# Attention and FFN on eight cores: heads and output tiles transposed by DMA, the first slab shared by four head pairs, side work planned by length

## The chip, the cores and the metric

The kernel runs on the eight NeuronCores of one Trainium2 chip. The cores work alone: no data passes between them. A core has TensorE (PE, matrix products), VectorE (DVE), ScalarE (ACT, here the exponentials), GpSimd (POOL) and SyncE (SP), each with its own instruction queue, and DMA queues that SP, POOL and ACT feed. Engines wait for each other by semaphores only. The metric is the device time of the slowest core, in microseconds.

## The reference, cut to what matters

```
x: (4, 4096, 1024)                      # 16 heads of width 64; one key and one value head for all
r = layernorm(x)
q = r @ query_proj   (per head)   k = r @ key_proj   v = r @ value_proj
o = softmax(q k^T / 8) v                # each head, 4096 keys
x = x + o @ output_proj
r = layernorm(x)
s = r @ Win + bin                       # 64 channels
g[m] = sum over h of relu(s[m] * W1[m,h] + b1[m,h]) * W2[m,h] + b2[m]     # 16 inner units
out = x + g @ Wout + bout
```

## The kernel before, in words

Two cores share one of the four sequences. Each computes keys and values for all 4096 rows (its own 2048, then the other core's), and outputs for its own. Matrices are bf16, sums f32.

The keys come in 32 tiles of 128 rows, four to a slab. A tile is loaded into `xbuf` (tiles 4 to 7 into `xtra`), DVE takes its statistics (`ln_stats`, L465), POOL makes 1/sqrt(var) in two steps (`rstd_of`, L833), DVE writes the normed bf16 tile `r1u` (`ln_norm`, L473), TensorE transposes it in eight 128x128 pieces into one of two side banks of PSUM (`sda`, `sdb`), and DVE copies it to `r1t`. A slab then gives keys (`K`, eight 512-column matmuls), values (`V`, 32 of 64 columns) and, for the core's own first four slabs, queries (`Q`, eight matmuls for a pair of heads). The core's 2048 queries are four stages k of 512; the 16 heads are eight pairs hp.

The main loop has 1024 groups. Group g takes one key tile, one head pair and 512 queries: two score matmuls on 64 rows (L662) into `spa` or `spb`, one exponential of 128x1024 on ACT (L816) into `ptu`, and eight P·V matmuls of 65 columns (L457; the 65th is the row sum) into `ob`. TensorE issues the scores of g+2 when exponential g is done, then P·V of earlier groups, eight or twelve at a time (`pv_at`). A slot is what stands on TensorE between the scores of one group and those of the next. `SEGS` (L32) is the order of the groups: stage 0 goes through the slabs as they come (the sums of a head pair are kept in `oacc` and DVE adds to them), stages 1 to 3 take each pair through all 32 tiles. At a pair's last group DVE normalises its output into `on` (`o_out`, L716).

All else is side work: a list `USES` (L120) of transposes (`tr`), keys, values, queries, transposed heads (`ot`: `on` to `ot`), output projections (`op`, `oq`), transposed output tiles (`rt`, from `r1u` to `r2t`), the FFN's first product (`s2`) and its second (`fo`). Each use takes the side bank that the use before last held, so TensorE waits at it for DVE's evacuation (`wait_ev`, semaphore `sev`). `pace` (L138) plans where the pieces stand among the groups, while the program is built: 2, 1 or 0 pieces in a slot with 0, 8 or 12 P·V matmuls, one DVE piece a slot, and, ahead of scores or P·V that need a key, value or query, everything up to it at once ("forced"). Engines run in order, so a piece that waits holds the scores behind it.

Stage k's projection and FFN run as side work of stage k+1. The last two output tiles are finished after the last exponential (the tail: `oq` leaves their last two head chunks to it). Result tiles are stored from POOL's queue, the next x tiles loaded from SP's (L895).

## Time and profile before

| | |
|---|---|
| median of 3 runs (lowest to highest) | 1017.74 us (1017.22 to 1017.86) |
| profiled execution, its own time | 1017.6 us |
| span of its slowest core; all cores | 1016.1 us; 1012.9 to 1016.1 us |
| ACT busy | 952.2 us, 94% of the span |
| PE busy, weight loads | 900.6 us (89%), 493.1 us (49%) |
| DVE busy | 358.7 us, 35% |
| granted clock of TensorE, all cores | 0.986 to 0.989 |

Busy time is the share of the span in which an engine had an instruction in work. ACT's exponentials overlap in the records: one is shown as lasting up to 1.2 us, while they start 0.9 us apart. The profiled execution's time is 1.5 us more than its slowest core's span, which is what lies around the program.

### The profile page before, as it was taken

What the parts mean: (1) busy time and instruction counts of PE and PEld (TensorE: products, weight loads), DVE (VectorE), ACT (ScalarE), POOL (GpSimd) and SP (SyncE); (2) the same over time, 40 slices, a digit from 0 to 9 for tenths busy, and PEclk for the clock granted to TensorE, in tenths of its full rate; (3) what the DMA queues carried; (4) which work ended last, traced back from release to release, by engine and by line L of the source; (5) the groups of instructions that cost most, each with busy time, mean ns of one, the idle gap of its engine ahead of it and who ended that gap; (6) DMA issues with size and microseconds to landing.
All of it is one profiled execution on the core that took longest, in us unless ns stands there. A gap on an engine that the chain in (4) does not pass through costs nothing.

```text
span 1016.1 us, 28595 instructions; the slowest of 8 cores (1012.9 to 1016.1 us)
## 1 busy us (share of the span) xinstructions
PE 900.6 (89%) x11582; PEld 493.1 (49%) x11712; DVE 358.7 (35%) x637; ACT 952.2 (94%) x1043; POOL 56.5 (6%) x131
## 2 busy tenths in 40 slices
PE   3898899998899999998889999998889998898884
PEld 3445555555444545544444454544444554454442
DVE  4535666652512222234202122244202326424215
ACT  2597999999999999999999999999999999999981
POOL 3201111100000000000000000000000000000000
...
GB/s 196 138 12 85 85 119 174 85 85 3 1 2 2 2 2 2 2 2 84 85 2 2 1 3 1 2 2 62 58 51 2 2 2 2 167 2 1 44 2 41
DMA packets 13406, 40.94 MB, mean 40 GB/s; under 512 B 3168, under 2 KB 3296, under 8 KB 13152
## 3 DMA queue, kind: packets, MB, share of 16 engines
...
q10 hardware_dynamic: 288, 0.52, 0.1%
...
## 4 chain that ended last, share of the span: by engine, by line
ACT 80%; issue 9%; PE 5%; DVE 3%; DMA 3%; POOL 0%; DVEq 0%; SPq 0%; POOLq 0%; ACTq 0%
ACT ptu L816 80%; DMA xtra<-x_own 2%; PE ob L457 1%; DMA xbuf<-x_own 1%; PE spa L662 1%; PE spb L662 1%; DVE r1u L478 1%; PE sda L380 0%; DVE r1t L504 0%; DVE lnst L468 0%; PE spb L695 0%; DVE lnst L469 0%; DVE gacc L787 0%; POOL rstd L838 0%; PE sdb L391 0%
## 5 line engine op out<-in xcount | busy, mean ns | idle before, releaser
L816 ACT ACTIVATE ptu<-spa 128x1024 bf16<-128x1024 f32 x512 | 594.5, 1161 | 17.7 <-PE spa L662 17.6
L816 ACT ACTIVATE ptu<-spb 128x1024 bf16<-128x1024 f32 x512 | 595.9, 1164 | 2.9 <-PE spb L662 2.9
L457 PE MATMUL ob<-vab,ptu 128*128 128x65 bf16 x8192 | 409.1, 195 | 0.7 <-ACT ptu L816 0.5
L457 PEld LDWEIGHTS ob<-vab,ptu 128*128 128x128 bf16 x8192 | 298.4, 97 | 208.4 <-issue 208.4
L662 PE MATMUL spb<-qt,k2t 64*128 64x512 bf16 x1024 | 200.8, 380 | 40.5 <-ACT ptu L816 34.9
L662 PE MATMUL spa<-qt,k2t 64*128 64x512 bf16 x1024 | 200.9, 380 | 36.5 <-ACT ptu L816 28.3
L662 PEld LDWEIGHTS spb<-qt,k2t 64*128 64x128 bf16 x1024 | 63.4, 92 | 127.2 <-issue 108.1
L662 PEld LDWEIGHTS spa<-qt,k2t 64*128 64x128 bf16 x1024 | 62.6, 92 | 114.5 <-issue 95.1
L725 DVE TENSOR_TENSOR oacc<-oacc,ob 128x520 f32<-128x520 f32 x50 | 34.8, 696 | 77.3 <-PE ob L457 77.2
L836 POOL TENSOR_SCALAR lnve<-lnmv 128x1 f32<-128x1 f32 x48 | 12.7, 264 | 658.0 <-DVE lnmv L471 658.0
L527 DVE TENSOR_TENSOR xbuf<-xbuf,sda 128x512 f32<-128x512 f32 x16 | 11.0, 688 | 93.3 <-PE sda L423 80.0
L527 DVE TENSOR_TENSOR xbuf<-xbuf,sdb 128x512 f32<-128x512 f32 x16 | 11.0, 688 | 89.5 <-PE sdb L423 54.9
L732 DVE RECIPROCAL zrec<-ob 128x8 f32<-128x8 f32 x24 | 5.0, 207 | 100.1 <-PE ob L457 99.8
L478 DVE TENSOR_SCALAR r1u<-xbuf,lnmv,rstd 128x1024 bf16<-128x1024 f32 x44 | 35.6, 810 | 9.1 <-POOL rstd L838 9.1
L423 PE MATMUL sda<-xtra,ot 128*128 128x512 bf16 x98 | 37.0, 379 | 0.0
L402 PE MATMUL sdb<-r1t,wqb 128*128 128x512 bf16 x104 | 35.9, 380 | 0.1
L423 PE MATMUL sdb<-xtra,ot 128*128 128x512 bf16 x96 | 35.4, 379 | 0.2 <-issue 0.2
L513 DVE CAST qt<-sdb 128x512 bf16<-128x512 f32 x16 | 11.0, 690 | 69.5 <-PE sdb L402 40.8
L402 PE MATMUL sda<-r1t,wqb 128*128 128x512 bf16 x96 | 34.4, 380 | 0.1
L468 DVE BATCH_NORM_STATS2 lnst<-xbuf 128x6 f32<-128x512 f32 x44 | 30.3, 689 | 10.9 <-DMA xbuf<-x_own 7.7
L513 DVE CAST qt<-sda 128x512 bf16<-128x512 f32 x15 | 10.3, 690 | 61.4 <-PE sda L402 42.9
L469 DVE BATCH_NORM_STATS2 lnst<-xbuf 128x6 f32<-128x512 f32 x44 | 29.7, 676 | 0.0
...
## 6 DMA issues: line engine op xcount, KB each, us to landing
xbuf<-x_own SPq DMA_DIRECT2D x28, 512.0 KB, 4.4
xbuf<-x_oth SPq DMA_DIRECT2D x16, 512.0 KB, 3.9
out<-xbuf POOLq DMA_DIRECT2D x14, 512.0 KB, 3.6
wqb<-wq POOLq DMA_DIRECT2D x8, 256.0 KB, 9.6
xtra<-x_own SPq DMA_DIRECT2D x4, 512.0 KB, 6.9
...
boutbc_s<-boutbc SPq DMA_DIRECT2D x1, 512.0 KB, 12.7
out<-xbuf SPq DMA_DIRECT2D x2, 256.0 KB, 2.6
```

What stands on the lines that cost most here:

```text
L402: r = te.matmul(bank[:], wqb[:, b, j, :], r1t[:, a, j, :], start=(j == 0), stop=(j == DCH - 1))
L423: r = te.matmul(bank[:], ot[:, blk % 2, c, t * 128:(t + 1) * 128], wpb[:, c, b * 512:(b + 1) * 512], start=(c == 0), stop=(c == heads - 1))
L457: r = te.matmul(osum[:, hd, c * 65:(c + 1) * 65], ptu[:, g % NPT, hd * 512 + c * 128:hd * 512 + (c + 1) * 128], vab[:, a + i, :], start=(i ...
L468: v.bn_stats(lnst[:, q, 0:6], xt(li)[:, 0:512])
L469: v.bn_stats(lnst[:, q, 6:12], xt(li)[:, 512:1024]).then_inc(bns, 1)
L478: v.tensor_scalar(r1u[:, li % 2, :], xt(li), lnmv[:, q, 0:1], rstd[:, q, :], op0=ALU.subtract, op1=ALU.mult).then_inc(nrm, 1)
L513: v.tensor_copy(qt[:, a % 2, b, :], bank[:]).then_inc(sev, 1)
L527: v.tensor_tensor(xh, xh, bank[:], op=ALU.add).then_inc(sev, 1)
L662: mm = te.matmul(sps[g % 2][:, hh * 512:(hh + 1) * 512], k2t[rows, mc * 128:(mc + 1) * 128], q, start=True, stop=True)
L725: v.tensor_tensor(oacc[:, hp], oacc[:, hp], osum, op=ALU.add).then_inc(oev, 1)
L816: sc.activation(ptu[:, g % NPT, :], sps[g % 2][:], AF.Exp, scale=0.125).then_inc(ex, 1)
L836: e.tensor_scalar(lnve[:, q, :], lnmv[:, q, 1:2], EPS, None, op0=ALU.add).then_inc(veps, 1)
```

## The change

1. Order of groups: head pairs 0 to 3 (before: 0 and 1) each go through slab 0 before slab 1 is used; pairs 4 to 7 then take both slabs at once. V0 comes ahead of the first scores; the queries of pairs 1 to 4 alternate with the transposes of slab 1; the keys of slab 1 are made in two pieces of 384 and 128 columns.
2. `r1u` has four buffers instead of two. Key tiles are transposed by TensorE as before.
3. Heads and output tiles are transposed by DMA on SP's queue (`head_transpose`, `tile_transpose`), in the order in which the plan notes them, except the very last head pair and the two tiles of the tail. Heads of stage 3 go in two halves. TensorE waits for their landing (`otl`, `trl`) at `op`, `oq` and `s2`; DVE waits before it writes a buffer of `on` or `r1u` again.
4. `pace` counts lengths in hundredths of a microsecond: a slot is 92, scores 22, half a P·V group 12, a piece 22, and pieces are added while TensorE's lag stays at or under 25. DVE's pieces have lengths too. A transposed head or tile counts as there six slots after its source.
5. The queries of stage 1 come at the end of stage 0, those of stage k+1 in stage k. The x tiles of later stages are loaded from POOL's queue, behind the stores; the projection's weights in eight loads instead of one.

```diff
-SEGS = [(0, 0, 0, 4), (0, 1, 0, 4), (0, 0, 4, 8), (0, 1, 4, 8)]
-SEGS += [(0, hp, 0, 8) for hp in range(2, NHP)]
+SEGS = [(0, hp, 4 * sl, 4 * sl + 4) for sl in range(2) for hp in range(4)]
+SEGS += [(0, hp, 0, 8) for hp in range(4, NHP)]
 SEGS += [(0, hp, 4 * sl, 4 * sl + 4) for sl in range(2, NSLAB) for hp in range(NHP)]
...
+    tr = slab(1)
+    o = [("V", 0, 0)] + q(0, 1) + tr[:1] + q(0, 2) + tr[1:2] + q(0, 3) + tr[2:3] + q(0, 4) + tr[3:]
+    o += [("V", 1, 0)] + q(0, 5, 6, 7)
     for s in range(2, NSLAB):
         o += slab(s) + [("V", s, 0)]
-    return o + q(1, 0) + [("ot", 0, hp) for hp in range(NHP - 1)]
+    return o + q(1, *range(NHP))
 
 
 def output_parts(b):
 
...
     fo = [("fo", 4 * b + t, h) for t in range(4) for h in range(2)]
-    return [op[0], op[1], rt[0:1] + op[2], rt[1:2] + op[3], rt[2:4], [("s2", b, 0)], fo[0:4], fo[4:8]]
+    return op + [[], [("s2", b, 0)], fo[0:4], fo[4:8]]
 
...
+SLOT = 92
+SCORES = 22
+SWITCH = 20
+HALF = 12
+PIECE = 22
+PE_LAG = 25
+TR_LAG = 6
...
+    def force(want, where):
+        n = 0
+        while not ok(want, -TR_LAG):
+            mm = [("smd", v) for name, v in want if name == "sev"]
+            if not ok(mm, 0) and ok(head["pe"], -TR_LAG):
+                run("pe", pe, "pe" + where)
+                n += 1
+            else:
+                assert head["dve"] is not None and ok(head["dve"][0], -TR_LAG), (now, head)
+                run("dve", dve, "dve" + where)
+        return n
+
+    pe_lag = dve_lag = 0
...
+            if last_part(s):
                 note("onr", 8 * SEGS[s][0] + SEGS[s][1] + 1)
-        while not ok(want, 0):
-            if head["pe"] is not None and ok(head["pe"], 0):
-                run("pe", pe, "pe0")
-            else:
-                assert head["dve"] is not None and ok(head["dve"], 0), (g, head)
-                run("dve", dve, "dve0")
+                note("otd", 8 * SEGS[s][0] + SEGS[s][1] + 1, TR_LAG)
...
+        forced += force([("sev", USE_NO["V", (SEGS[s][2] + h // 2) // 4, 0] + 1) for h in halves], "_v")
+
+        pe_lag = min(pe_lag + PIECE * forced, PE_LAG)
+        t = SCORES + HALF * len(halves) + (SWITCH if halves or forced else 0)
+        switch = 0 if halves or forced else SWITCH
+        while head["pe"] is not None and ok(head["pe"], 1):
+
+            if pe_lag + t + switch + PIECE - SLOT > (PE_LAG if g >= 14 else 75):
+                break
+            run("pe", pe, "pe")
+            t += switch + PIECE
+            switch = 0
+        pe_lag = max(0, pe_lag + t - SLOT)
+
+        room = SLOT + (20 if g + 1 in SEG_AT else 115)
+        while head["dve"] is not None and ok(head["dve"][0], 1) and dve_lag + head["dve"][1] <= room:
+            dve_lag += head["dve"][1]
+            run("dve", dve, "dve")
+        dve_lag = max(0, dve_lag - SLOT)
+    return counts, moves
 
 
...
+                                         r1u[:, a % 4, j * 128:(j + 1) * 128], identb[:])
                 elif kind == "K":
-                    yield [("sev", n)]
-                    wait_ev(te, n - 1)
-                    for j in range(DCH):
-                        if j:
-                            yield []
-                        r = te.matmul(bank[:], wkb[:, j, :], r1t[:, slab_buf(a), j, :],
-                                      start=(j == 0), stop=(j == DCH - 1))
+
+                    parts = [(0, 3), (3, 4)] if a == 1 else [(0, 4)]
+                    for t0, t1 in parts:
+                        tr = USE_NO["tr", 4 * a + t1 - 1, 0]
+                        cols = slice(128 * t0, 128 * t1)
+                        for j in range(DCH):
+                            if j == 0:
+                                yield [free, ("sev", tr + 1)]
+                                wait_ev(te, n - 2)
+                                wait_ev(te, tr)
+                            elif j % (4 if t1 - t0 == 1 else 1) == 0:
+                                yield []
+                            r = te.matmul(bank[:, cols], wkb[:, j, :], r1t[:, slab_buf(a), j, cols],
+                                          start=(j == 0), stop=(j == DCH - 1))
                 elif kind == "V":
                     yield [free]
...
-                    yield [free, ("sev", done + 1)]
+
+                    done = 8 * blk + ({12: 3, 14: 6}[a // 2 * 2] if blk == LAST else NHP - 1)
+                    yield [free, ("otd", done + 1)]
...
+                    li = NTILES + GROUPS[a][-1]
+                    yield [free, ("trd", li + 1)]
                     if a == 0:
                         te.wait_ge(winl, 16)
-                    wait_ev(te, n - 1)
+                    wait_ev(te, n - 2)
...
 
 
-        def ln_stats(v, li):
+        def ln_stats_a(v, li):
             q = li % 4
             wait_x(v, li)
             v.bn_stats(lnst[:, q, 0:6], xt(li)[:, 0:512])
+
+        def ln_stats_b(v, li):
+            q = li % 4
...
-            if 2 <= li < 6:
-                v.wait_ge(ptr, li - 1)
-            v.tensor_scalar(r1u[:, li % 2, :], xt(li), lnmv[:, q, 0:1], rstd[:, q, :],
+            if 4 <= li < 8:
+                v.wait_ge(ptr, li - 3)
+            elif li < NTILES + 4:
+
+                if li >= 8:
+                    v.wait_ge(smd, USE_NO["tr", li - 4, 0] + 1)
+            else:
...
                 r.then_inc(kmm, 1)
-            te.wait_ge(pset, 1)
-            te.wait_ge(qev, 2)
             for g in range(-2, NG):
-                run(gen, counts["pe0"].get(g, 0))
+                run(gen, counts["pe_s"].get(g, 0))
+                if g == -2:
+                    te.wait_ge(pset, 1)
+                    te.wait_ge(qev, 2)
...
+                    v.wait_ge(otl[n % 2], heads_moved(n - 2))
                 v.reciprocal(zrec[:, n % 2], src[:, :, :, 64:65]).then_inc(rcp, 1)
...
+                    c = i - 24
                     e.wait_ge(nrm, 8)
-                    e.dma_start(wpb, wp_d.rearrange("p (c d) -> p c d", d=D)).then_inc(wpl, 16)
+                    e.dma_start(wpb[:, c, :], wp_d[:, c * D:(c + 1) * D]).then_inc(wpl, 16)
             for ts in GROUPS[:-1]:
                 for t in ts:
...
+                        e.wait_ge(ost[t % 4], 16 * (t // 4 + 1))
+                        e.dma_start(xbuf[:, t % 4, :], xo_r[t + 4]).then_inc(xol[t % 4], 16)
             for t in GROUPS[-1]:
                 rstd_of(e, NTILES + t)
...
+        def tile_transpose(e, li, dst):
+            e.wait_ge(nrm, li + 1)
+            e.dma_start_transpose(dst, r1u[:, li % 4, :]).then_inc(trl[li % 4], 16)
+
+        def head_transpose(e, k, i):
+
+            n = 8 * k + i
+            if i == 0 and k >= 2:
+                wait_ev(e, USE_NO["op", 4 * (k - 2) + 3, 1])
+            e.wait_ge(onr, n + 1)
+            if k < LAST:
+                e.dma_start_transpose(ot[:, k % 2, i, :].rearrange("p (c t) -> p c t", c=4),
+                                      on[:, n % 2].rearrange("p c t -> p (c t)")).then_inc(otl[n % 2], 16)
+            else:
+                q0 = 256 * (i // 4)
+                for c in range(2):
+                    e.dma_start_transpose(
+                        ot[:, k % 2, 2 * (i % 4) + c, q0:q0 + 256].rearrange("p (c t) -> p c t", c=2),
+                        on[:, n % 2, 2 * c:2 * c + 2].rearrange("p c t -> p (c t)")).then_inc(otl[n % 2], 16)
 
         @block.sync
         def _(e):
@@ -892,10 +986,15 @@
...
-                for t in range(4):
-                    e.wait_ge(ost[t], 16 * k)
-                    e.dma_start(xbuf[:, t, :], xo_r[4 * k + t]).then_inc(xl[t], 16)
+            for kind, n in moves:
+                if kind == "otd":
+                    if n < 8 * NK - 1:
+                        head_transpose(e, n // 8, n % 8)
+                    continue
+                t = n - NTILES
+                if t == GROUPS[GROUP_OF[t]][0]:
+                    wait_ev(e, USE_NO["s2", GROUP_OF[t] - 1, 0] if t else USE_NO["V", 6, 0])
+                tile_transpose(e, n, r2t[:, :, t % 4 * 128:t % 4 * 128 + 128])
             for n, t in enumerate(GROUPS[-1]):
                 e.wait_ge(oad, 2 * n + 1)
                 e.dma_start(out_r[t][:, 0:512], xbuf[:, t % 4, 0:512]).then_inc(osp, 16)

```

TensorE's queue at the start, ahead of the first scores that need slab 1; before (L662 scores, L457 P·V, L372 transposes, L380 keys, L391 values, L402 queries):

```order
L662 MATMUL spb<-qt,k2t 128x512 x2
L457 MATMUL ob<-vab,ptu 128x65 x12
L372 MATMUL sdb<-identb,r1u 128x128 x8
L372 MATMUL sda<-identb,r1u 128x128 x8
L372 MATMUL sdb<-identb,r1u 128x128 x8
L380 MATMUL sda<-r1t,wkb 128x512 x8
L391 MATMUL sdb<-wvb,r1t 128x64 x32
L662 MATMUL spa<-qt,k2t 128x512 x2
L457 MATMUL ob<-vab,ptu 128x65 x12
L662 MATMUL spb<-qt,k2t 128x512 x2
L457 MATMUL ob<-vab,ptu 128x65 x8
```

After, the piece of head pair 3 that ends in the first scores of slab 1 (L727 scores, L513 P·V, L453 queries, L415 transposes, L430 keys):

```order
L453 MATMUL sdb<-r1t,wqb 128x512 x2
L727 MATMUL spa<-qt,k2t 128x512 x2
L453 MATMUL sdb<-r1t,wqb 128x512 x4
L727 MATMUL spb<-qt,k2t 128x512 x2
L513 MATMUL ob<-vab,ptu 128x65 x12
L453 MATMUL sdb<-r1t,wqb 128x512 x2
L415 MATMUL sda<-identb,r1u 128x128 x8
L430 MATMUL sdb<-r1t,wkb 128x384 x8
L430 MATMUL sdb<-r1t,wkb 128x128 x8
L727 MATMUL spa<-qt,k2t 128x512 x2
```

What stood ahead of the ninth group's scores stands ahead of the seventeenth's. The values have gone behind them, and queries of the next pair have come in between.

TensorE's queue ahead of slab 2; before (row L380 is the key matmul of slab 2):

```order
L372 MATMUL sda<-identb,r1u 128x128 x4
L662 MATMUL spa<-qt,k2t 128x512 x2
L457 MATMUL ob<-vab,ptu 128x65 x8
L372 MATMUL sda<-identb,r1u 128x128 x4
L662 MATMUL spb<-qt,k2t 128x512 x2
L457 MATMUL ob<-vab,ptu 128x65 x8
L372 MATMUL sdb<-identb,r1u 128x128 x8
L380 MATMUL sda<-r1t,wkb 128x512 x8
L391 MATMUL sdb<-wvb,r1t 128x64 x32
L662 MATMUL spa<-qt,k2t 128x512 x2
```

After, the keys of slab 2, which begin eleven groups before the sixty-fifth group's scores:

```order
L430 MATMUL sda<-r1t,wkb 128x512 x2
L727 MATMUL spa<-qt,k2t 128x512 x2
L513 MATMUL ob<-vab,ptu 128x65 x8
L430 MATMUL sda<-r1t,wkb 128x512
L727 MATMUL spb<-qt,k2t 128x512 x2
L513 MATMUL ob<-vab,ptu 128x65 x8
L430 MATMUL sda<-r1t,wkb 128x512
L727 MATMUL spa<-qt,k2t 128x512 x2
L513 MATMUL ob<-vab,ptu 128x65 x8
L430 MATMUL sda<-r1t,wkb 128x512
L727 MATMUL spb<-qt,k2t 128x512 x2
L513 MATMUL ob<-vab,ptu 128x65 x8
```

The keys of slab 2 and its values have moved from one slot into a dozen.

DVE's queue in the new start, between the query cast of pair 1 and that of pair 2 (L583 query casts, L789 copy of the sums, L574 copy of a transposed tile, L524 to L530 statistics, L547 norm):

```order
L583 CAST qt<-sdb 128x512 [waits sem_side_mm]
L789 COPY oacc<-ob 128x520 [waits sem_pv_mm]
L574 COPY r1t<-sda 128x8x128 [waits sem_side_mm]
L524 BN_STATS lnst<-xtra 128x6 [waits sem_xtra_load2]
L528 BN_STATS lnst<-xtra 128x6
L530 BN_AGGR lnmv<-lnst 128x2 [waits sem_bn_stats]
L547 TENSOR_SCALAR r1u<-xtra,lnmv,rstd 128x1024 [waits sem_rstd_set,sem_first_transposed]
L583 CAST qt<-sdb 128x512 [waits sem_side_mm]
```

The cast of the next query stands behind a tile's statistics and another's norm; in the old order these stood among transposes.

## Rows read from the trace of the kernel before

**Rows 1.** The page: the chain that ended last, shares of the span by engine.
```profile
ACT 80%; issue 9%; PE 5%; DVE 3%; DMA 3%; POOL 0%; DVEq 0%; SPq 0%; POOLq 0%; ACTq 0%
```

**Rows 2.** ACT's waits (total us, times, longest), 24 to 62 us, then 62 to 1000.
```profile
ACT ptu L816 <- PE spa L662: 10.4, 4, 6.6
ACT ptu L816 <- PE spb L662: 1.9, 1, 1.9
...
ACT ptu L816 <- PE spa L662: 7.1, 3, 6.3
ACT ptu L816 <- PE spb L662: 1.0, 2, 0.8
```

**Rows 3.** ACT in order of time: start us, duration us, instruction [idle before].
```profile
24.18 1.02 ACT L816 ACTIVATE ptu<-spa 128x1024 bf16<-128x1024 f32 x1 [0.32 <-PE spa L662]
...
51.27 1.02 ACT L816 ACTIVATE ptu<-spa 128x1024 bf16<-128x1024 f32 x1 [2.06 <-PE spa L662]
...
93.27 1.20 ACT L816 ACTIVATE ptu<-spa 128x1024 bf16<-128x1024 f32 x1
94.18 1.20 ACT L816 ACTIVATE ptu<-spb 128x1024 bf16<-128x1024 f32 x1
101.67 1.02 ACT L816 ACTIVATE ptu<-spa 128x1024 bf16<-128x1024 f32 x1 [6.29 <-PE spa L662]
...
984.56 1.20 ACT L816 ACTIVATE ptu<-spb 128x1024 bf16<-128x1024 f32 x1
```

**Rows 4.** All engines in order of time, 22 to 27 us: the first scores, V0.
```profile
22.88 0.61 PE L635 MATMUL ob<-r1t,wkb 128*128 128x128 bf16 x8
...
23.70 0.39 PE L662 MATMUL spa<-qt,k2t 64*128 64x512 bf16 x2 [0.20 <-DVE qt L756]
...
25.68 1.11 PE L391 MATMUL sda<-wvb,r1t 128*128 128x64 bf16 x32
```

**Rows 5.** All engines, 38 to 42 us, and two rows near 87 us.
```profile
38.56 1.67 PE L380 MATMUL sda<-r1t,wkb 128*128 128x512 bf16 x7 [1.16 <-DVE r1t L504]
...
40.34 0.69 DVE L508 CAST k2t<-sda 128x512 bf16<-128x512 f32 x1 [2.14 <-PE sda L380]
...
41.29 0.39 PE L662 MATMUL spa<-qt,k2t 64*128 64x512 bf16 x2
...
41.62 0.54 PE L457 MATMUL ob<-vab,ptu 128*128 128x65 bf16 x12
...
42.09 0.39 PE L662 MATMUL spb<-qt,k2t 64*128 64x512 bf16 x2
...
86.68 0.42 PE L457 MATMUL ob<-vab,ptu 128*128 128x65 bf16 x8
...
86.94 0.39 PE L372 MATMUL sda<-identb,r1u 128*128 128x128 bf16 x4
```

**Rows 6.** The page's groups: busy us, mean ns of one, idle before.
```profile
L402 PE MATMUL sdb<-r1t,wqb 128*128 128x512 bf16 x104 | 35.9, 380 | 0.1
...
L468 DVE BATCH_NORM_STATS2 lnst<-xbuf 128x6 f32<-128x512 f32 x44 | 30.3, 689 | 10.9 <-DMA xbuf<-x_own 7.7
...
L478 DVE TENSOR_SCALAR r1u<-xbuf,lnmv,rstd 128x1024 bf16<-128x1024 f32 x44 | 35.6, 810 | 9.1 <-POOL rstd L838 9.1
```

**Rows 7.** The page's DMA issues: count, KB each, us from issue to landing.
```profile
xbuf<-x_own SPq DMA_DIRECT2D x28, 512.0 KB, 4.4
...
wqb<-wq POOLq DMA_DIRECT2D x8, 256.0 KB, 9.6
```

**Rows 8.** A stretch: us, PE, PEld, DVE, ACT, POOL busy, PEclk, DMA share, GB/s.
```profile
95.00:102.00 7.00, 5.02 (x51) 2.93 (x52) 4.80 (x10) 0.71 (x2) 1.56 (x4) 0.76 0.15 60
```

**Rows 9.** All engines: the keys of slab 2; the last P·V; the last norm.
```profile
96.98 3.00 PE L380 MATMUL sda<-r1t,wkb 128*128 128x512 bf16 x7 [2.10 <-DVE r1t L504]
...
985.90 0.41 PE L457 MATMUL ob<-vab,ptu 128*128 128x65 bf16 x8 [0.52 <-ACT ptu L816]
...
986.73 0.69 DVE L734 TENSOR_TENSOR on<-ob,zrec 128x512 bf16<-128x512 f32 x1
```

184 lines of the change are left out of this document (92 added, 92 removed).

## The prediction

> **What bounds the kernel now.** The page's head gives the slowest core a span of 1016.1 us, in an execution of 1017.6 us; 80% of the chain that ended last is the exponential of line 816 on ACT [rows 1]. Before a share is trusted, the stage behind it is to be read: the exponentials stand 0.91 to 0.92 us apart when nothing disturbs them (93.27 to 94.18), the first starts at 24.18, the last at 984.56 [rows 3]. 1024 of them at that step are 939 us, and no part of the change touches the step. What is left is 24 us ahead of the first, 30 us behind the last, whose code is the same but for buffer indices, and the holes. ACT's waits say where those are: 10.4 + 1.9 us before 62 us, 7.1 + 1.0 us after it [rows 2]. In order of time the reader sees two places: the seventeenth exponential (slab 1 is done by then) starts at 51.27, where a hole-free run would have it at 24.18 + 14.7 = 38.9; and the sixty-fifth, the first that needs slab 2, comes 7.49 us after its predecessor, 6.3 of them idle [rows 3]. All other holes are 7.1 + 1.0 - 6.3 = 1.8 us. So at most 20.4 us can be had, whatever DVE and PE shed elsewhere.
>
> **The change, part by part.**
> *V0 ahead of the first scores.* The first scores started at 23.70, having waited for a query cast [rows 4]. The key matmuls before them started at 22.88 and take 0.61 - 0.17 = 0.44 of TensorE's time (0.17 is what one 512-column matmul's 0.38 [rows 6] is over the step of 0.21 that seven in 1.67 show [rows 5]). V0's 32 matmuls then run from 23.3 for 1.11 - 0.17 = 0.94 [rows 4], the scores start at 24.3, and the first exponential 0.48 later: 24.8, +0.6.
> *First slab used by four head pairs.* Per pair the new order on TensorE, by the steps of [rows 5]: scores 0.33 (41.29 to 41.62) four times, twelve P·V twice 0.47 (41.62 to 42.09), eight P·V 0.26 (86.68 to 86.94), eight transposes 0.5, eight query matmuls 1.7, the last one's end 0.17: 4.9 us. The next pair's scores wait for that query's cast: 0.1, then 0.69, and 0.26 until TensorE goes on (40.34 + 0.69 to 41.29). DVE is later still: ahead of that cast stand the copy of the sums, the transposed tile's copy, statistics (two at 0.69 and an aggregate, 1.6) and a norm (0.81) [rows 6], 3.8 us that can begin 1.5 us after the scores, so the cast starts at 5.3 instead of 5.0. A period is 6.3 us for four exponentials, where their own time is 3.7. The first pair: the scores of its fourth key tile wait for five query matmuls, those of pair 1 for DVE, which has two tiles of statistics and a norm before the cast (24.5 + 0.4 + 3.2 + 0.8 + 0.7 + 0.3 = 29.9): the fifth exponential is at 30.4. The ninth 36.7, the thirteenth 43.0. Then TensorE's queue holds the last transposes and both pieces of key matmuls: 5.0 + 0.7 + 0.3 for the query's cast, 8 x 0.16 for 384 columns, 0.44 for 128, 0.2, cast 0.69, 0.26, to which 0.2 comes for the hop: 8.8, so the seventeenth is at 51.8. Before: 51.27. So this part loses 0.6 in all, V0 included: the four pairs give work to ACT, but each query is asked for just before its use. Unknown is what late weights do: query chunk 3 is issued near 27.8 and needed at 38.1, 10.3 us for a transfer whose median is 9.6 [rows 7]; from nothing to 2 us.
> *V1.* 24 matmuls (0.7) and then P·V that waits for their cast: 0.8 in place of 0.33. Two slots take 2.3 against 1.83; an exponential after a hole lasts 1.02 and in the steady stretch 1.20 [rows 3], so 0.18 of lateness is free. +0.3.
> *Slab 2 planned.* In the order of before, eight transposes, eight key and 32 value matmuls stand in one slot ahead of the scores that need slab 2. In the new order they are spread from slot 40 to 62, the last key matmul six slots before its use. The 6.3 us go. What is late next there is nothing I find: 8 P·V with one piece is 0.33 + 0.26 + 0.21 = 0.8, below 0.917. Of the 1.8 us in other holes, made by the same kind of forced pieces, I take 1.0 as gained; bounds 0 and 1.8.
> *Pieces by length.* From slot 16 on there are now 79 slots with 12 P·V and a piece (none before) and 75 with 8 P·V and two (one with more before). They cost 0.33 + 0.47 + 0.21 = 1.01 and about 0.33 + 0.26 + 0.43 = 1.02, 0.1 over a slot; the plan's own lag may reach 0.25, 0.07 beyond the free 0.18. No row has such a slot, so bounds: nothing, since lighter slots follow, and 75 x 0.07 = 5 us. I take 0.3, near the lower end, because the lag counted is seldom at its top.
> *Heads and output tiles by DMA.* 31 head and 14 tile transposes leave TensorE and DVE; both wait for ACT in those stages, so this brings nothing. What replaces them are 52 transposing transfers on SP's queue (38 of heads, those of stage 3 in halves, and 14 of tiles), in the order of the plan; SP stands still at each until its source is written, and behind it only further transposes wait, the loads of x having gone to POOL's queue. POOL there holds the next tiles' rstd behind the stores' landing and four loads, each about the 4.4 us of a 512 KB load [rows 7], with over 30 slots before that rstd is wanted. The price is a wait on TensorE, with scores queued behind it. The last P·V of a stage stands 8 slots (7.3 us) before the first projection; reciprocal and norm end 1.1 after that P·V's 0.41 (985.90 to 987.42 [rows 9]), and in stage 0 the sum costs another 0.8. That leaves 5.4 us once (stage 0) and 6.2 four times. Tiles: 5.9 before the third FFN and 5.0 before the fourth (11 and 9 slots less 4.2 and 3.2, with POOL's two steps and hops estimated at 1.1), over 10 before the others. A head is 128 KB, a tile 256 KB. The nearest rows are plain loads of 512 KB at 4.4 and, in the crowd of the start, 9.6 for half that [rows 7]. I take 4.4 as the likelier, since in these stages the queues are near empty: no wait. The other end, 9.6, costs 4.2 + 4 x 3.4 + 3.7 + 4.6 = 26 us.
> The Trainium skill disagrees with itself here. "VectorE: DVE Perf Modes", section "The three transpose paths", gives the DMA crossbar 1.31 us for 128x128 where TensorE has 0.39. If blocks add up, an estimate from that page is 5.2 us for a head and 10.5 for a tile. "DMA: Bandwidth & Descriptors", section "Anatomy of one DMA", gives a fixed 2 us and the bytes at 436 GB/s; an estimate by that is 2.3 and 2.6 us, and then no wait at all. No row here shows a transposing transfer; by the first page the sum would be rival C, by the second the forecast.
>
> **Sum.** +0.6 (start) + 0.3 (V1) - 6.3 (slab 2) - 1.0 (small holes) + 0.3 (heavy slots) + 0 (transfers) = -6.1. The profiled execution was 1017.6, so 1011.5; the median of the runs is 0.1 above it: 1011.7 us. The unknowns at their best (all small holes, DVE 0.5 earlier in each of the first periods, heavy slots nothing) give 1009; and if the start hides one more cast, 1007.5.
>
> **Rivals.**
> A. The start costs more than worked out: a query's weights land 2 us late, or TensorE's granted clock falls in the first 52 us. For it: it fell in the hole before slab 2, to 0.76 on the mean of 95 to 102 [rows 8], and the new start has gaps of 1.3 us in each period. Against: the larger hole before 41 us cost no clock. In that stretch the seven key matmuls took 3.00 [rows 9] where 1.67 is usual [rows 5], so 1.3 per such fall. Time: 1011.7 + 2 to 3, 1014.
> B. The heavier slots are not absorbed: +5 as bounded above, 1016.5. For it: 154 such slots. Against: none exceeds a slot by more than 0.1.
> C. Slower: transposing transfers outlast the plan. With one length L for all, the seven close waits cost (L - 5.4) + 4(L - 6.2) + (L - 5.9) + (L - 5.0) = 7L - 41; that passes the gain of 6.1 from L = 6.7. At twice the plain load, 8.8, it is 20.5 and the time 1032. It is worse if they also don't overlap, for the heads of stage 0 come every 3.7 us: at 5.2 each, the last of eight lands 11 us late, DVE waits for the buffer of normed heads, and with tiles at 10.5 (4.6 + 5.5) the sum is +21, again 1032. For it: no row of this kernel shows such a transfer at all. Against: twice to four times the bytes land in 4.4.
> D. The change doesn't remove the wait for slab 2 but meets it elsewhere, since the same 48 exponentials must cover the same tiles. Against: slots 16 to 62 have 36 us and the pieces need under 25. It is taken with A.
>
> **Chances.** Forecast 0.66 (its own range 1009 to 1014), A with D 0.14, B 0.07, C 0.13. A measurement tells 0.2%, 2.0 us, from no change. Faster by more: all but a little of the forecast, two thirds of A, a quarter of B: 0.77. Same: 0.10. Slower: C, 0.13. The range reaches up over A and B to 1018.5 and down to 1007.5; C is left out.
>
> **What would show it.** The first exponential at 24.8, the fifth near 30.4, the seventeenth near 51.8; no hole over 1 us at the sixty-fifth; the last near 978.5; holes by ACT's waits near 14 in all; head transfers under 5.4 us from issue to landing and no wait of TensorE at the first projections; steady step 0.917 still. It would be wrong if the seventeenth came 3 us from 51.8, if the step in the middle stages grew, or if a transposing transfer took over 6 us.

## The result, and the profile after

The changed kernel takes 1029.54 us (median of 4 runs, 1028.76 to 1029.84); the kernel before took 1017.74 in the same comparison. The ratio is 1.0116 with an interval of 1.0096 to 1.0136: slower by 11.8 us, where 6.1 us less had been forecast. The profiled execution has a span of 1027.2 us on its slowest core (all cores 1020.5 to 1027.2), 11.1 more than before. Some executions of any kernel run with the cores of one die at a lower clock and take some per cent longer; the times and ratios of this document leave them out.

The chain of the page, by engine, answers to [rows 1]; the two groups of exponentials follow (busy us, mean ns of one, idle before).

```profile
ACT 47%; PE 34%; issue 8%; DVE 7%; DMA 2%; DVEq 0%; SPq 0%; POOL 0%; ACTq 0%; POOLq 0%
...
L885 ACT ACTIVATE ptu<-spa 128x1024 bf16<-128x1024 f32 x512 | 552.7, 1079 | 19.5 <-PE spa L727 17.6
L885 ACT ACTIVATE ptu<-spb 128x1024 bf16<-128x1024 f32 x512 | 553.2, 1081 | 2.9 <-PE spb L727 2.8
```

ACT has 47% of the chain where it had 80%, PE 34% where it had 5%. And an exponential's mean duration fell from 1.16 us (the mean over the trace of before) to 1.08. That is bad news here: the records of neighbours overlap while ACT has the next one waiting, so a short record is one that was fed late.

ACT's waits, from 24 to 62 us and from 62 to 1000, answer to [rows 2].

```profile
ACT ptu L885 <- PE spa L727: 12.2, 9, 4.6
ACT ptu L885 <- PE spb L727: 1.1, 4, 0.3
...
ACT ptu L885 <- PE spa L727: 5.4, 11, 1.7
ACT ptu L885 <- PE spb L727: 1.7, 7, 0.3
ACT ptu L885 <- issue: 0.8, 4, 0.2
```

Behind 62 us the waits are 7.9 us where they were 8.1. By this view nothing was lost there. The starts of the exponentials tell another story. In order of time, answering to [rows 3]:

```profile
25.10 1.02 ACT L885 ACTIVATE ptu<-spa 128x1024 bf16<-128x1024 f32 x1 [1.46 <-PE spa L727]
...
52.63 1.02 ACT L885 ACTIVATE ptu<-spa 128x1024 bf16<-128x1024 f32 x1 [4.58 <-PE spa L727]
...
96.61 1.07 ACT L885 ACTIVATE ptu<-spb 128x1024 bf16<-128x1024 f32 x1
97.70 1.03 ACT L885 ACTIVATE ptu<-spa 128x1024 bf16<-128x1024 f32 x1
...
995.51 1.09 ACT L885 ACTIVATE ptu<-spb 128x1024 bf16<-128x1024 f32 x1
```

The hole ahead of slab 2 is gone: 97.70 is the sixty-fifth exponential, 1.09 behind its predecessor instead of 7.49. Counting exponentials from 0, the two kernels compare so, each in its slowest core:

| stretch | before, us | after, us | difference |
|---|---|---|---|
| span's start to exp 0 | 24.18 | 25.10 | +0.9 |
| exp 0 to 16 | 27.09 | 27.53 | +0.4 |
| exp 16 to 64 (slab 2 is needed) | 50.39 | 45.07 | -5.3 |
| exp 64 to 256 | 177.55 | 181.36 | +3.8 |
| exp 256 to 1023 | 705.34 | 716.45 | +11.1 |
| exp 1023 to the end | 31.5 | 31.7 | +0.2 |

What had been planned was gained by exp 64 and lost threefold behind it. To see where, each step between two exponentials from 256 on was sorted by what TensorE had in its queue between their scores, and the excess over 0.917 us added up: 57 slots of eight P·V with two pieces ran 1.057 us each, +8.0; 73 slots of twelve P·V alone 0.984, +4.9, where the 97 of before had 0.916; 242 slots of eight P·V with one piece 0.916, nothing. These are two mechanisms. The sums are gross: they hold single waits as well (one step of 2.26 us among the 57 is a wait for a transposed tile), and the steps behind a late exponential run under 0.917 and give part back. What each mechanism cost net is read from the experiments.

**The lead of ACT.** All engines but the weight loads, in the steady part of stage 1:

```profile
307.02 1.06 ACT L885 ACTIVATE ptu<-spb 128x1024 bf16<-128x1024 f32 x1
...
307.34 0.39 PE L727 MATMUL spa<-qt,k2t 64*128 64x512 bf16 x2
307.67 0.41 PE L513 MATMUL ob<-vab,ptu 128*128 128x65 bf16 x8
307.92 0.59 PE L476 MATMUL sda<-xtra,ot 128*128 128x512 bf16 x2
307.92 1.07 ACT L885 ACTIVATE ptu<-spa 128x1024 bf16<-128x1024 f32 x1
308.44 0.39 PE L727 MATMUL spb<-qt,k2t 64*128 64x512 bf16 x2
...
308.94 1.02 ACT L885 ACTIVATE ptu<-spb 128x1024 bf16<-128x1024 f32 x1
309.86 1.02 ACT L885 ACTIVATE ptu<-spa 128x1024 bf16<-128x1024 f32 x1
310.76 1.03 ACT L885 ACTIVATE ptu<-spb 128x1024 bf16<-128x1024 f32 x1
...
311.43 0.60 PE L476 MATMUL sda<-xtra,ot 128*128 128x512 bf16 x2
...
311.66 1.05 ACT L885 ACTIVATE ptu<-spa 128x1024 bf16<-128x1024 f32 x1
```

The two pieces at 307.92 put the next scores 1.10 us behind the last (307.34 to 308.44), and the exponential that needs them comes 1.02 after its predecessor and lasts 1.02. From there the durations creep up, 1.02, 1.03, 1.05, while the starts stand 0.90 to 0.92 apart. ACT fully fed is at 1.20 and 0.917 [rows 3]. So the 0.18 of lateness is there, but it comes back at about 0.0125 us per exponential, 14 of them for all of it, and the next slot of two pieces stood four to six slots on (here at 311.43), where only a part had come back. In the stretches without such slots it did come back: 196 of the 768 exponentials from 256 on last 1.19 us or more, where 568 did before.

That ACT itself sets this pace, and not TensorE, shows where the slots hold eight P·V alone:

```profile
469.64 1.03 ACT L885 ACTIVATE ptu<-spa 128x1024 bf16<-128x1024 f32 x1
469.90 0.39 PE L727 MATMUL spb<-qt,k2t 64*128 64x512 bf16 x2 [0.17 <-ACT ptu L885]
470.54 1.05 ACT L885 ACTIVATE ptu<-spb 128x1024 bf16<-128x1024 f32 x1
470.81 0.39 PE L727 MATMUL spa<-qt,k2t 64*128 64x512 bf16 x2 [0.17 <-ACT ptu L885]
471.44 1.06 ACT L885 ACTIVATE ptu<-spa 128x1024 bf16<-128x1024 f32 x1
```

TensorE waits for ACT before each pair of scores, and ACT's starts still stand 0.90 apart while its durations grow by 0.01 to 0.02.

**The clock.** The windows of all engines around the end of a segment (columns as in [rows 8]; the third number from the end is the granted clock), and TensorE in order of time:

```profile
427.00:431.00 4.00, 3.30 (x42) 1.78 (x42) 0.23 (x2) 4.00 (x5) 0.00 (x0) 1.00 0.00 0
431.00:433.00 2.00, 0.95 (x11) 0.43 (x10) 0.67 (x1) 2.00 (x4) 0.00 (x0) 0.99 0.03 8
433.00:436.00 3.00, 3.00 (x40) 1.94 (x36) 0.00 (x0) 2.67 (x4) 0.00 (x0) 0.50 0.17 38
```

```profile
431.58 0.39 PE L727 MATMUL spb<-qt,k2t 64*128 64x512 bf16 x2 [0.52 <-ACT ptu L885]
432.50 0.39 PE L727 MATMUL spa<-qt,k2t 64*128 64x512 bf16 x2 [0.53 <-ACT ptu L885]
432.82 0.76 PE L513 MATMUL ob<-vab,ptu 128*128 128x65 bf16 x12
433.51 0.60 PE L727 MATMUL spb<-qt,k2t 64*128 64x512 bf16 x2
```

TensorE had two slots with scores alone, 431 to 433: it was busy 0.95 of 2 us. Then the granted clock stood at 0.50, which is 1.2 GHz, for some 3.4 us. These held the segment's three slots of twelve P·V, which ran 1.23, 1.32 and 1.19 us. It happened five times from exp 256 on (at 282, 433, 463, 671 and 702 us), about 1.0 us each, each right behind such a pair of slots. The trace has 12 pairs from exp 256 on in the changed kernel (the expectations count 13, and 16 in e1, where the trace has 10), because the planner has done the work early, and one in the kernel before, where no core's clock fell between exp 256 and 1023. The eight cores run the same program, and the clock fell in them three to six times in that stretch, always behind one of the pairs, but not the same ones: behind the pair at exp 450 in seven cores, behind that at 738 in one. The cores with three falls took 714.0 to 714.2 us from exp 256 to 1023, those with six 716.8. The Trainium skill, "TensorE: Matmul & The Clock Gate", section "Part 1: The HAM clock gate", says that the clock is gated to 1.2 GHz by how busy TensorE has been; the trace agrees in the level, 0.50. The program alone doesn't decide whether a given pair is followed by a fall, since the cores differ.

The transfers were as quick as hoped. The DMA issues of the page (SPq, us from issue to landing), for [rows 7]:

```profile
ot<-on SPq DMA_TRANSPOSE x38, 2.4
...
r1t<-r1u SPq DMA_TRANSPOSE x14, 3.1
```

### The profile page after: what moved, and what is told of

Its sections match the earlier page's. It is cut to its first block, busy times and chain, and to the rows that moved or that the text cites. A ratio compares the mean times of both kernels' runs of the same rounds, so it can differ in the third digit from the quotient of the medians.

```text
span 1027.2 us, 28339 instructions; the slowest of 8 cores (1020.5 to 1027.2 us)
## 1 busy us (share of the span) xinstructions
PE 901.2 (88%) x11484; PEld 472.0 (46%) x11484; DVE 339.5 (33%) x594; ACT 961.5 (94%) x1043; POOL 73.4 (7%) x150
## 2 busy tenths in 40 slices
DMA packets 46284, 48.65 MB, mean 47 GB/s; under 512 B 35152, under 2 KB 35280, under 8 KB 46160
## 4 chain that ended last, share of the span: by engine, by line
ACT 47%; PE 34%; issue 8%; DVE 7%; DMA 2%; DVEq 0%; SPq 0%; POOL 0%; ACTq 0%; POOLq 0%
ACT ptu L885 47%; PE ob L513 12%; PE spa L727 6%; PE spb L727 6%; PE sdb L476 2%; PE sda L476 2%; PE sdb L453 1%; DVE hr L640 1%; DVE hz L636 1%; PE sda L453 1%; DVE gacc L650 1%; PE sda L430 1%; DMA wvb<-wv 1%; DMA xbuf<-x_own 1%; DVE lnst L524 1%
## 5 line engine op out<-in xcount | busy, mean ns | idle before, releaser
L885 ACT ACTIVATE ptu<-spa 128x1024 bf16<-128x1024 f32 x512 | 552.7, 1079 | 19.5 <-PE spa L727 17.6
L885 ACT ACTIVATE ptu<-spb 128x1024 bf16<-128x1024 f32 x512 | 553.2, 1081 | 2.9 <-PE spb L727 2.8
L513 PE MATMUL ob<-vab,ptu 128*128 128x65 bf16 x8192 | 412.5, 196 | 1.1 <-ACT ptu L885 0.7
L513 PEld LDWEIGHTS ob<-vab,ptu 128*128 128x128 bf16 x8192 | 301.6, 98 | 211.0 <-issue 211.0
L727 PE MATMUL spa<-qt,k2t 64*128 64x512 bf16 x1024 | 201.3, 385 | 45.5 <-ACT ptu L885 37.4
L727 PE MATMUL spb<-qt,k2t 64*128 64x512 bf16 x1024 | 201.9, 387 | 43.0 <-ACT ptu L885 40.3
L727 PEld LDWEIGHTS spa<-qt,k2t 64*128 64x128 bf16 x1024 | 56.0, 93 | 140.7 <-issue 132.6
L727 PEld LDWEIGHTS spb<-qt,k2t 64*128 64x128 bf16 x1024 | 56.0, 93 | 136.3 <-issue 126.5
L905 POOL TENSOR_SCALAR lnve<-lnmv 128x1 f32<-128x1 f32 x48 | 18.0, 374 | 759.5 <-DVE lnmv L530 759.4
L453 PE MATMUL sdb<-r1t,wqb 128*128 128x512 bf16 x144 | 47.4, 380 | 0.0
L476 PE MATMUL sdb<-xtra,ot 128*128 128x512 bf16 x124 | 43.6, 379 | 0.0
L476 PE MATMUL sda<-xtra,ot 128*128 128x512 bf16 x124 | 43.1, 379 | 0.0
L547 DVE TENSOR_SCALAR r1u<-xbuf,lnmv,rstd 128x1024 bf16<-128x1024 f32 x44 | 35.6, 810 | 15.3 <-POOL rstd L907 15.3
L453 PE MATMUL sda<-r1t,wqb 128*128 128x512 bf16 x104 | 36.1, 380 | 0.0
L524 DVE BATCH_NORM_STATS2 lnst<-xbuf 128x6 f32<-128x512 f32 x44 | 30.2, 687 | 11.0 <-DMA xbuf<-x_own 7.8
L907 POOL TENSOR_TENSOR rstd<-lnve,mhalf 128x1 f32<-128x1 f32 x48 | 27.7, 577 | 7.1
L583 DVE CAST qt<-sdb 128x512 bf16<-128x512 f32 x18 | 12.4, 690 | 28.0 <-PE sdb L453 27.9
```

Source lines behind the costliest of these rows:

```text
L453: r = te.matmul(bank[:], wqb[:, b, j, :], r1t[:, a, j, :], start=(j == 0), stop=(j == DCH - 1))
L476: r = te.matmul(bank[:], ot[:, blk % 2, c, t * 128:(t + 1) * 128], wpb[:, c, b * 512:(b + 1) * 512], start=(c == 0), stop=(c == heads - 1))
L513: r = te.matmul(osum[:, hd, c * 65:(c + 1) * 65], ptu[:, g % NPT, hd * 512 + c * 128:hd * 512 + (c + 1) * 128], vab[:, a + i, :], start=(i ...
L524: v.bn_stats(lnst[:, q, 0:6], xt(li)[:, 0:512])
L547: v.tensor_scalar(r1u[:, q, :], xt(li), lnmv[:, q, 0:1], rstd[:, q, :], op0=ALU.subtract, op1=ALU.mult).then_inc(nrm, 1)
L727: mm = te.matmul(sps[g % 2][:, hh * 512:(hh + 1) * 512], k2t[rows, mc * 128:(mc + 1) * 128], q, start=True, stop=True)
```

## The experiments

Three theories were put against each other: **1**, slots heavier than ACT's step cost ACT its lead; **2**, idle slots cost TensorE its clock; **3**, the transposing DMAs, with some 32,000 small packets, slow the engines. (The expectations say 35,000; the pages have 35,152 packets under 512 B in the changed kernel and 3,168 before.) The ratios are to runs of the kernel before in the same series, where it took about 1019 us.

**e1_strict.** The lateness allowed to TensorE.

```diff
-PE_LAG = 25
+PE_LAG = 0
```

> The changed kernel with the planner's allowed lateness for TensorE set from 25 to 0 hundredths of a microsecond from slot 14 on. Between the 256th and the last exp, 57 slots held eight P·V and two pieces and 24 held twelve P·V and one; now none and 19. Theory 1 (pieces): in the changed kernel the 57 slots ran 1.057 us each against 0.917, 8.0 us in all, because ACT regains only 0.0125 us per exp after it was fed late. All of that goes, and 1.9 us of the 12 such slots before the 256th exp: 1029.5 - 9.9 = about 1019.6 (1017 to 1022). Theory 2 (clock): the granted clock fell to 0.50 five times, each right behind two slots in which TensorE had scores alone; there are 16 such pairs now (13 before), so the five drops of 1.0 us each stay or become 3 to 8: this part alone leaves 1028 to 1032. Theory 3 (the 52 transposing DMAs with their 35,000 small packets disturb the engines): nothing changes, 1029. Both 1 and 2 hold in my view, so 1020, with at least three clock drops.

Measured: 1023.41 us, ratio to the kernel before 1.0048 (1.0016 to 1.0079). The time from exp 256 to 1023 fell from 716.45 to 710.16, by 6.3. The clock fell to 0.50 four times in it, each time behind a pair of empty slots. The 6.3 is not the two-piece slots alone: one fall and the wait for a tile went with them, and a wait of 1.4 us for a head came. Theory 1 holds for about half of the loss, theory 2 stands, theory 3 is out as the main cause.

**e2_repeat.** The scores twice where TensorE has nothing else.

```diff
-                    for hh in range(2):
+                    bare = g >= 0 and not pv_at(SEG_OF[g], g - SEG_AT[SEG_OF[g]]) and not any(
+                        counts[w].get(g, 0) for w in ("pe_s", "pe_v", "pe"))
+                    for hh in [0, 1, 0, 1] if bare else [0, 1]:
```

> The changed kernel with the two score matmuls issued twice, with the same operands and the same result, in every slot that holds neither P·V nor a piece (46 slots, among them 13 pairs of neighbours). It adds 0.2 us of work to TensorE where it idles for 0.8 us. Theory 2 (clock): TensorE no longer idles through two slots running, the five drops to 0.50 between the 256th and the last exp vanish, and with them 4.9 us: about 1024.7 (1023.5 to 1026). If the drops have nothing to do with the idle slots: 1029.5 or slightly more, and the drops are still there. Theories 1 and 3 have no part in it.

Measured: 1025.37 us, ratio 1.0062 (1.0044 to 1.0079); exp 256 to 1023 in 711.46, 5.0 less. The same stretches as above, in this kernel:

```profile
430.00:432.00 2.00, 1.52 (x16) 0.64 (x18) 0.90 (x2) 2.00 (x3) 0.00 (x0) 1.00 0.00 0
432.00:435.00 3.00, 2.55 (x37) 1.31 (x34) 0.00 (x0) 3.00 (x4) 0.00 (x0) 1.00 0.22 49
```

The clock stays at 1.00, here and at all 12 pairs, in all eight cores, and the 73 slots of twelve P·V run 0.908 us. More work for TensorE, of no use to anybody, saved 5 us. Some of that is the wait for a tile near exp 842, whose step is 1.1 us shorter here; the falls themselves cost 0.8 to 0.9 us net each, by the cores with three and with six of them against the 711.46 to 711.68 of the eight cores here.

**e3_strict_repeat.** Both edits.

> Both edits: allowed lateness 0, and repeated scores in the slots that are otherwise empty. If 1 and 2 are separate and complete, the losses of 8.0, 1.9 and 4.9 us all go: about 1029.5 - 14.8 = 1014.7 (1012.5 to 1017), faster than the kernel before by about 3 us. Under theory 3 it stays above 1024.

Measured: 1019.75 us, ratio 1.0018 (0.9991 to 1.0045): no slower than before, but not the 3 us faster either. Exp 256 to 1023 took 707.45, 9.0 less than in the changed kernel, and in seven cores, the slowest among them, no clock fell in it (in one it fell behind a wait of 1.3 us for a head). Both mechanisms are real, but the two gains (6.3 and 5.0) don't add up in full, and in the slowest core 2.1 us of the 11.1 were still open. The three cores with the shortest time took 706.10 to 706.13 here, 5.4 less than the cores of e2: that is what the strict allowance brings by itself. Two candidates: six slots whose steps were 1.9 us long in excess and which hold a piece that waits for VectorE's adds, and one wait of 1.4 us for a transposed head. e6 and e7 take one each.

**e4_before_two.** The kernel before, with the suspected cost put in.

```diff
-        for _ in range({0: 2, 2: 1, 3: 0}[halves]):
+        for _ in range({0: 2, 2: 2, 3: 0}[halves]):
```

> The kernel before, with two pieces allowed in a slot of eight P·V in place of one; nothing else is changed, no DMA transposes. 233 slots after the 256th exp and some 30 ahead of it now hold eight P·V and two pieces, mostly with slots of eight P·V and none between them. Theory 1: every such slot costs ACT 0.10 to 0.14 us, about 264 x 0.12 = 32 us: 1050 (1040 to 1058). The planner's reckoning (a slot of 1.10 us followed by one of 0.66 us costs nothing, as 0.18 us of lateness is free): 1018. Theory 3: 1018 as well.

Measured: 1057.87 us, ratio 1.0383 (1.0365 to 1.0401), 38 us more between exp 256 and 1023 for 233 such slots. No transposing DMA is in it, so theory 3 isn't needed. But most of them stand in unbroken runs of 1.10 us, where lateness must add up by anybody's reckoning; how fast the lead comes back it doesn't tell. The next two do.

**e9_sixteenth** and **e10_fourth.** The kernel before, with a second piece in every 16th or every 4th slot (`g % 16 == 8`, `g % 4 == 0`).

```diff
-        for _ in range({0: 2, 2: 1, 3: 0}[halves]):
+        for _ in range({0: 2, 2: 2 if g % 16 == 8 else 1, 3: 0}[halves]):
```

> The kernel before, with a second piece allowed in every 16th slot of eight P·V alone: 30 slots behind the 256th exp hold eight P·V and two pieces, each with at least 15 others between it and the next. If ACT's 0.18 us of lead is lost to such a slot and regained at 0.0125 us per exp (14 exps), a slot that has 15 behind it costs nothing: the time of the kernel before, within 0.5 us (30 slots at their full 0.18 would be 5.4 us). If a two-piece slot costs 0.14 us wherever it stands: 4.2 us more.

> The same with every 4th slot: 89 such slots behind the 256th exp, mostly four slots apart. Three other slots give back 3 to 4 x 0.0125 = 0.05 us of the 0.18, so each costs 0.13 to 0.14 us: 89 x 0.135 = 12 us more than the kernel before (9 to 14), less for the first of each run of them. By the planner's reckoning (0.18 us of lateness, of which a slot with one piece gives 0.04 back and one with none 0.26) some runs of two-piece slots exceed the allowance slightly, and 2 us more would be the most. Here the slots are four apart in both readings; what differs is how fast the lead comes back.

Measured: 1020.14 us, ratio 1.0018 (1.0003 to 1.0032), and 1026.18 us, ratio 1.0086 (1.0061 to 1.0111). From exp 256 to 1023: 706.18 and 713.19, +0.8 and +7.9 on the kernel before. The first is near no cost (30 slots at 0.14 would be 4.2), if above the 0.5 that I had allowed. In the second, 19 of the 89 slots are the first of their run and find the lead built up; the other 70 cost 0.11 each. The four steps of such a round, 1.04, 0.92, 0.90 and 0.91, are 0.10 over four of 0.917. My 12 was too high: I took the slot at 1.05 and more, and the first ones with the rest. ACT with one such slot in 16, then with one in 4:

```profile
306.62 1.12 ACT L816 ACTIVATE ptu<-spb 128x1024 bf16<-128x1024 f32 x1
307.52 1.13 ACT L816 ACTIVATE ptu<-spa 128x1024 bf16<-128x1024 f32 x1
308.56 1.02 ACT L816 ACTIVATE ptu<-spb 128x1024 bf16<-128x1024 f32 x1
```

```profile
304.31 1.04 ACT L816 ACTIVATE ptu<-spa 128x1024 bf16<-128x1024 f32 x1
305.35 1.02 ACT L816 ACTIVATE ptu<-spb 128x1024 bf16<-128x1024 f32 x1
...
308.07 1.04 ACT L816 ACTIVATE ptu<-spa 128x1024 bf16<-128x1024 f32 x1
309.12 1.02 ACT L816 ACTIVATE ptu<-spb 128x1024 bf16<-128x1024 f32 x1
```

The heavy slot's step is the same 1.04 in these rows. What differs is what it takes away: a duration of 1.13, built up before it, or one of 1.04, where hardly any lead had come back. The ends of the exponentials tell it for all such slots: in their steps the ends stood 0.93 us apart on the mean with one in 16, and 0.99 with one in 4, where a fed ACT has 0.917.

**e12_before_empty.** The kernel before, with the other suspected cost put in.

```diff
-        for _ in range({0: 2, 2: 1, 3: 0}[halves]):
+        for _ in range({0: 2 if g < 256 else 0, 2: 1, 3: 0}[halves]):
```

> The kernel before, with no piece allowed in the two slots without P·V that begin each segment behind slot 256: 24 pairs of slots in which TensorE has scores alone, where the kernel before has one. The work goes into slots of eight P·V (one piece each), and 16 matmuls more are left behind the last exp. Theory 2 (clock): behind some of the pairs the granted clock falls to 0.50 and three steps run 1.0 us long in all; 5 of 13 pairs did so in the changed kernel, so about 9 drops and 9 us from the 256th to the last exp over the 705.3 us of the kernel before (3 to 20 us). If idle slots have no part in the drops: 705 us and none.

Measured: 1023.62 us, ratio 1.0048 (1.0034 to 1.0061). Three falls of the clock from exp 256 on, at 756, 875 and 964 us, each behind one of the 24 pairs, steps up to 1.32 in all three; the 12-P·V slots lost 2.9 us where they had lost nothing. Exp 256 to 1023 took 707.07, only 1.7 more, since two holes of the kernel before (steps of 1.61 and 1.41) are not in this one. The rest of what this run has over the kernel before is 1.3 behind the last exp and what lies ahead of exp 256, where nothing was changed. One of the stretches:

```profile
754.00:756.00 2.00, 0.95 (x6) 0.30 (x6) 0.80 (x2) 2.00 (x3) 0.00 (x0) 1.00 0.84 336
756.00:759.00 3.00, 3.00 (x36) 1.83 (x35) 0.00 (x0) 2.61 (x4) 0.00 (x0) 0.53 0.26 85
```

In these stages of the two kernels the clock never fell but behind an idle pair, and repeating the scores prevents it, but it fell behind 3 of 24 here and behind 5 of 12 there (in all eight cores 23 of 192 and 34 of 96). The pairs concerned differ from core to core here too. What decides among them, beside the program, stays open, and with it the size: my 9 was three times too many.

**e5_double.** Every transposing DMA twice, on e3's kernel.

```diff
             e.dma_start_transpose(dst, r1u[:, li % 4, :]).then_inc(trl[li % 4], 16)
+            if li > NTILES:
+                e.wait_ge(trl[(li - 1) % 4], 32 * ((li - 1 - NTILES) // 4 + 1))
+            e.dma_start_transpose(spare[:], r1u[:, li % 4, :]).then_inc(trl[li % 4], 16)
...
```

SP here also waits until the transfers of the head or tile before have landed, which the kernel of e3 doesn't: where they land late, the next one is late as well.

> The kernel of e3_strict_repeat with each of the 52 transposing DMAs issued twice, the second into a spare tile; whoever waits for a transfer waits for both. Theory 3 (the transposing DMAs and their small packets slow the engines, in e3 too): the part of the time that they cost is paid twice; if they are why e3 is no faster than the kernel before (3 to 5 us short), it goes to about 1023 to 1025. If they cost nothing but a late landing: the one wait for a head in the last block (1.4 us at exp 905) grows by the 2.4 us that a transfer took, and all else stays: 1019.7 to 1022, and from exp 16 to exp 896 the time is that of e3 (814.4 us) within 0.5 us.

Measured: 1024.38 us, ratio 1.0065 (1.0042 to 1.0088), in the range of the first reading by the total, but the two readings differ in where the time goes, so the stretches must decide. From exp 256 to 896, where heads and tiles are moved all the time, it took 589.66 us, e3 589.44: twice the packets cost 0.2. (Ahead of the first transposing DMA, at 255.7 us, the two differ by 0.8 already.) The rest is behind exp 896, 123.20 against 118.01. There the clock fell twice: at 970 behind a wait of 1.3 us for the heads, now doubled, and at 875 behind a stall of TensorE of 1.6 us in the middle of a P·V group, which the profile puts down to nothing ("issue"), while x loads and the heads were in flight together. Whether the doubled transfers made that one stays open; the kernel before has no such stall there. In four other cores TensorE waited 1.5 to 2.1 us for a doubled head at the same place, and the clock fell behind it. As a steady cost theory 3 is out; a transfer costs by landing late, and in this core both stalls were followed by a fall of the clock (in two other cores a wait of 1.4 to 1.5 us was not).

**e7_lag8.** Landing planned 8 slots behind the issue (`TR_LAG = 8`).

> The kernel of e3_strict_repeat with the landing of a transposing DMA planned 8 slots behind its issue in place of 6. In e3 TensorE waited once, 1.4 us, for a head of the last block, and the step at exp 905 was 2.32 us. If the plan's 6 slots are too few there, the wait goes: 1018.4. The two matmuls of a piece more that now stand behind the last exp may cost 0.4 back. If the transfer is late for another reason, the wait is still there: 1019.7.

Measured: 1023.55 and 1026.17 us, with no ratio for two runs; the first has a span of 1021.7 us. The wait did not go, it grew, and all eight cores have it (2.7 to 5.4 us), where three had it in e3. DMA issues from 862 to 886 us, then TensorE's wait:

```profile
xbuf<-x_own POOLq DMA_DIRECT2D x4, 512.0 KB, 7.8
...
ot<-on SPq DMA_TRANSPOSE x2, 9.0
```

```profile
PE sdb L476 <- DMA ot<-on: 3.9, 1, 3.9
```

The two half heads took 9.0 us where 2.4 is the median, with four x loads of 512 KB, newly on POOL's queue, in flight beside them. In e3 they took 6.4, with a wait of 1.4; in e6, where these loads are issued 9 us later, 2.3, with none. Behind the 3.9 us the clock stood at 0.50 for 6.8 us: the step at exp 907 was 5.25 us, the next three 1.52, 1.53 and 1.34. The cause was not a landing planned too soon but the loads in flight with it, and my expectation was wrong.

**e6_dve_room.** VectorE's allowed lateness 20 instead of 115.

> The kernel of e3_strict_repeat with the planner's allowed lateness of VectorE set from 115 to 20 hundredths of a microsecond in all slots (20 was the value for the last slot of a segment only). In e3 the steps of six slots in which a piece waited for VectorE (exps 436, 437, 449, 661, 879 and 883) were 1.13 to 1.48 us, 1.9 us over 0.917 in all. If the allowance makes them, they go: about 1018 (1017 to 1019.5). If the waits come from the pieces' own order (two adds of 0.69 us per output half), nothing changes: 1019.7.

Measured: 1017.09 us, ratio 0.998 (0.997 to 0.999). Exp 256 to 1023 took 705.34 us in the slowest core, by chance to the hundredth that of the kernel before; the other seven took 704.7, where every core of the kernel before has 705.3. The waits for VectorE are gone, and with the x loads later also the one for a head: 706.1 to 704.7, 1.4 us. So the 11.1 us of the middle stages are found again: about 5 for the clock (with a wait for a tile), 5.4 for the slots, 1.4 for VectorE's pieces, less the 0.6 by which these stages now beat the kernel before.

**e8_all** and **e11_best.** Two pieces allowed where they help, up to slot 60; e6's edits; `TR_LAG` 8 and 6.

```diff
-            if pe_lag + t + switch + PIECE - SLOT > (PE_LAG if g >= 14 else 75):
+            if pe_lag + t + switch + PIECE - SLOT > (75 if g < 14 else PE_LAG if g < 60 else 0):
...
```

> All that the runs point to: lateness of TensorE allowed as in the changed kernel up to slot 60 and none behind it, scores repeated in empty slots, VectorE's allowance 20, transfers planned 8 slots ahead. The changed kernel had its 64th exp at 97.70, e3 at 100.96, of which 1.2 us was a clock drop at 37 us; so about 2 us from the start, 1.5 from VectorE and 1.0 from the transfer, against e3: 1019.0 - 4.5 = 1014.5 (1012 to 1017), faster than the kernel before by 2 to 5 us. If the gains of the start are given back by exp 256, as in the changed kernel against the kernel before, 1016.5.

> The kernel of e8_all with transfers planned 6 slots ahead again, as in the changed kernel (e6_dve_room had no wait for a head with 6). e8 lost 3.1 us at exps 204 to 206 to a stall of 1.4 us with a clock drop behind it, in its profiled run. About the time of e8, 1013 to 1015, or 0.4 us less for the two matmuls that no longer stand behind the last exp.

Measured: 1015.12 us, ratio 0.9962 (0.9948 to 0.9976), and 1015.98 us, ratio 0.9972 (0.9961 to 0.9983): both beat both kernels, by 3 to 4 us against the kernel before, and don't differ from each other beyond their intervals. The chain of e11_best:

```profile
ACT 78%; issue 10%; PE 8%; DVE 2%; DMA 1%; POOL 0%; DVEq 0%; SPq 0%; POOLq 0%; ACTq 0%
```

ACT is back at 78%; exp 1023 starts at 981.14, 3.4 before that of the kernel before.

## Why the prediction was wrong

*V0, and the first slab used by four pairs:* right. First exponential 25.10 (24.8 forecast), fifth 30.83 (30.4), ninth 37.31 (36.7), thirteenth 43.39 (43.0), seventeenth 52.63 (51.8). The part loses 1.4 instead of 0.6. A part of that was an error of adding: the terms from the thirteenth to the seventeenth come to 9.1, not 8.8, and 9.2 was measured.

*V1 and slab 2 planned:* right, -5.3 from the seventeenth to the sixty-fifth with V1 in it, where -6.0 was the sum of the two terms. The hole did not reappear elsewhere (rival D). But 1.5 of the 5.3 is a fall of the clock in the hole of before, which two of its eight cores had; the other six took 48.9 us for this stretch, and gain 3.9.

*Small holes, -1.0:* not gained. From exp 64 to 256 the change lost 3.8 in the slowest core; 48 slots of twelve P·V with a piece cost 2.0 gross and 12 of two pieces 1.9. Another 1.9 is one stall of TensorE of 1.8 us at 197 us, put down to nothing ("issue"), which four cores don't have: they took 179.4, about 2 more than the 177.3 to 178.0 that are common before. What made the stall stays open.

*Pieces by length, +0.3:* the step that failed. Right was that ACT stands 0.18 of lateness. Wrong was "since lighter slots follow": I let the 0.18 come back with the next light slot, as the planner does. It comes back at 0.0125 us per exponential. So what counts is the distance between heavy slots, 14 for nothing, and not the lag's top. The slot was too short in the sum as well: 1.02 where 1.10 was measured from scores to scores, and 0.8 where 0.89 was for eight P·V with one piece; the planner's own numbers, 110 and 88 hundredths, were right. The term was 5.4 us from exp 256 on (e3 against e2) and 2.8 from exp 64 to 256 (176.6 in e3's and e1's undisturbed cores, 179.4 in the changed kernel's): 8.2, where 0.3 stood. My upper bound of 5 had the same error in it, and rival B with it: the right mechanism at some 60% of its size and a chance of 0.07. The sign that I had named came: from exp 256 on the mean step is 0.934, where it was 0.920.

*Missing altogether:* the clock in the middle stages, 4 to 5 us in the slowest core. Rival A had the price of a fall nearly right (1.3; it is 1.0 in the three steps, 0.8 to 0.9 net) but looked for it at the start alone, and its "Against" held for one core only: in another core of the kernel before the clock did fall, at 37 us. Missing too were VectorE's late pieces, 1.4 us. That work which is done early leaves empty slots later could be read from the plan.

*Heads and tiles by DMA:* right; 2.4 and 3.1 us against my 4.4, and one wait of 1.0 us, for a tile that took 4.4 beside two half heads. Of the Trainium skill's two estimates, that from "VectorE: DVE Perf Modes", "The three transpose paths", 5.2 and 10.5 with blocks added up, is refuted; that from "DMA: Bandwidth & Descriptors", "Anatomy of one DMA", 2.3 and 2.6, fits the head and is 0.5 short for the tile, though the section is on DMAs that GpSimd issues and these come from SyncE. Rival C's mechanism exists (9.0 us in e7), but by crowding, not by the transfer's own length.

Also nearly right was that freeing TensorE and DVE of these transposes brings nothing in the middle stages: e6, without them, is within 0.6 us of the kernel before. The sum over the stretches then is 1.4 - 5.3 + 3.8 + 11.1 + 0.2 = +11.2, the span's difference, against -6.1.
